# One 64x64 block-diagonal stationary tile for two 32-row quarters in the small levels of a triangular inversion

## The reference

```python
A = jnp.where(tri, 0.0, -jnp.einsum('bhncd,bhned->bhnce', kb, k))     # layer 0; kb = k * beta
for i in range(1, chunk):
    upd = jnp.einsum('...k,...kj->...j', A[..., i, :], A[..., :, :i])
    A = A.at[..., i, :i].add(upd)
inv = A + jnp.eye(chunk, dtype=A.dtype)                               # inverse of a unit lower triangular matrix
u, w = inv @ v, inv @ kb
# then chunk by chunk: out = q S + attn (u - w S);  S = S + k^T (u - w S)
```

## Time and profile before

| | |
|---|---|
| median of 3 runs | 6088.86 us |
| lowest and highest run | 6067.7 and 6097.42 us |
| span of the profiled execution, first to last instruction | 6065.7 us |
| instructions in it | 101127 |
| mean granted TensorE clock, of full speed | 0.739 |
| busy: PE, PEld, DVE, ACT, POOL | 66%, 50%, 54%, 32%, 13% |

### The profile page before, as it was taken

The page is one execution under the profiler, slowest core; times in us unless marked ns, Lnnn a source line. Parts: engine busy times, 40 slices in busy tenths (PEclk is TensorE's granted clock), DMA queues, the critical chain, the costliest instruction groups (busy, mean ns, idle before and its releaser), DMA issues.

```text
span 6065.7 us, 101127 instructions
## 1 busy us (share of the span) xinstructions
PE 4010.7 (66%) x42763; PEld 3031.6 (50%) x42812; DVE 3278.0 (54%) x8153; ACT 1942.4 (32%) x4236; POOL 818.4 (13%) x600
## 2 busy tenths in 40 slices
PE   5565656367778787755475665657767677766288
PEld 4454535255555555544353544534444445445277
DVE  6776867425555555565446455455565555555332
ACT  2233231223333333311313233234444444442122
POOL 0000000231111111124200000011111111110444
PEclk6555555588898988866666666668887788778599
DMA  9000000140000000011200000000000000000255
GB/s 256 15 2 1 2 1 2 61 143 1 1 1 1 1 1 1 1 35 19 47 2 1 2 1 1 2 1 1 1 1 1 1 1 1 1 1 1 66 160 142
DMA packets 140741, 148.57 MB, mean 24 GB/s; under 512 B 7792, under 2 KB 127986, under 8 KB 139776
## 3 DMA queue, kind: packets, MB, share of 16 engines
q1 hardware_dynamic: 118880, 124.05, 7.0%
q0 software_dynamic: 21408, 18.05, 1.8%
HBM read 83.22 MB, written 59.76 MB: 24 GB/s over the span
## 4 chain that ended last, share of the span: by engine, by line
PE 43%; DVE 35%; ACT 12%; issue 6%; POOL 2%; DMA 2%; another core or an unknown queue 1%; SPq 0%; DVEq 0%; POOLq 0%; ACTq 0%
DVE weights L1215 4%; ACT work L3162 4%; PE banks_lane L422 3%; PE banks_lane L3599 2%; PE banks_lane L1818 2%; PE banks_lane L3004 2%; PE banks_lane L3048 2%; DVE weights L3255 1%; PE banks_lane L933 1%; ACT work L1912 1%; PE banks_lane L3083 1%; DVE work L2725 1%; PE banks_lane L793 1%; PE banks_lane L3070 1%; PE banks_lane L1876 1%
## 5 line engine op out<-in xcount | busy, mean ns | idle before, releaser
L422 PE MATMUL banks_lane<-constants,weights 128*128 128x128 f32 x724 | 154.3, 358 | 492.7 <-DVE weights L408 135.2
L422 PE MATMUL banks_lane<-constants,work 128*128 128x128 f32 x840 | 171.1, 351 | 356.8 <-DVE work L408 195.0
L422 PEld LDWEIGHTS banks_lane<-constants,weights 128*128 128x128 f32 x724 | 111.6, 184 | 532.5 <-issue 170.9
L402 POOL TENSOR_TENSOR weights<-weights,constants 128x4 f32<-128x4 f32 x80 | 82.6, 1033 | 2169.4 <-DVE weights L397 2169.4
L1215 DVE SCALAR_TENSOR_TENSOR weights<-weights 128x1024 f32<-128x1024 f32 x268 | 342.4, 1278 | 6.8
L422 PEld LDWEIGHTS banks_lane<-constants,work 128*128 128x128 f32 x840 | 132.3, 182 | 423.4 <-DVE work L408 185.4
L3162 ACT ACTIVATE work<-banks_lane,weights 128x192 f32<-128x192 f32 (+1 forms) x512 | 248.6, 499 | 245.6 <-DVE weights L3259 245.6
L3267 POOL TENSOR_TENSOR weights<-weights,constants 128x16 f32<-128x16 f32 x64 | 185.5, 2898 | 530.8 <-DVE weights L3175 530.8
L402 POOL TENSOR_TENSOR work<-work,constants 128x4 f32<-128x4 f32 x72 | 73.4, 1020 | 1171.0 <-DVE work L397 1171.0
L3083 PE MATMUL banks_lane<-constants,work 128*128 128x128 f32 x896 | 149.6, 316 | 120.5 <-DVE work L3247 70.8
L1965 DVE TENSOR_REDUCE work<-banks_lane 128x2 f32<-128x512 f32 x256 | 158.8, 683 | 67.6 <-PE banks_lane L1832 67.2
(11 more groups left out here) (795 smaller groups left out, 10922.9 us busy)
## 6 DMA issues: line engine op xcount, KB each, us to landing
work<-experts_dram_l_ffn SPq DMA_DIRECT2D x39, 964.0 KB
room_l_ffn<-work SPq DMA_DIRECT2D x30, 1188.0 KB, 14.1
work<-experts_dram_l_ffn SPq DMA_DIRECT2D x23, 512.0 KB
weights<-weights_dram SPq DMA_DIRECT2D x1, 4833.5 KB, 14.1
work<-room_l_ffn SPq DMA_DIRECT2D x36, 132.0 KB
weights<-weights_dram SPq DMA_DIRECT2D x1, 4112.0 KB, 12.4
weights<-room_l_ffn SPq DMA_DIRECT2D x26, 132.0 KB
weights<-weights_dram SPq DMA_DIRECT2D x1, 3378.0 KB, 10.8
```

The costliest lines, as they stand in the source:

```text
L402: pool.tensor_tensor(n.rstd, n.rstd, c("neghalf", cols=(0, n.rstd.shape[1])), ALU.pow).then_inc(*u.pool.step(name))
L422: done = pe.transpose(bank[0:rows, t * P:(t + 1) * P], block, c("ident"))
```

## The change

In levels 1 to 4 two neighbouring quarters share one stationary tile of 64x64, whose two off-diagonal 32x32 blocks are zero. A product is then, for each of the 8 matrices, two matmuls instead of four. The moving operand stays 32 columns wide in the left product and 16 in the right one, but covers 64 partitions. `strict` gets its own storage, 512 columns, cleared once at the start, with the four copies of `strict_act` going into alternate halves of it. The masked part is written 64 columns wide for each matrix (`part_pair`): the left product's result is read twice by a broadcast, and the masks `small1` to `small4` are 64 wide with zeros where the other quarter lies. Level 0 first adds the two halves of `strict`, one of which is zero on each quarter, to get its 32 columns. Level 5 and 6 are as before.

```diff
-        parts += [(f"small{n}", np.tile(m.T if n == 0 else m, (4, 1)))]
+        parts += [(f"small{n}", np.tile(m.T, (4, 1)) if n == 0 else np.tile(np.kron(np.eye(2), m), (2, 1)))]
...
+def half_of(g):
+    return slice(2 * g * SMALL, 2 * (g + 1) * SMALL)
...
-        self.part, self.strict = (blocks(whole(self.T1)[:, n * small:(n + 1) * small], SMALL) for n in range(2))
+        self.strict = arena.take(INVERTED, 2 * SMALL)
+        self.strict_half = [self.strict[:, :, n * SMALL:(n + 1) * SMALL] for n in range(2)]
+        self.part = blocks(whole(self.T1)[:, 0:small], SMALL)
+        self.part_pair = blocks(whole(self.T1)[:, 0:2 * small], 2 * SMALL)
...
         dve.memset(self.XT, 0.0).then_inc(*u.dve.step())
+        dve.memset(self.strict, 0.0).then_inc(*u.dve.step("strict_cleared"))
...
             for m in range(INVERTED):
-                for q in map(quarter, range(QUARTERS)):
-                    made = pe.matmul(b[2][q, m * SMALL:(m + 1) * SMALL], self.strict[q, m, :], self.x[q, m, :])
+                for g in map(half_of, range(2)):
+                    made = pe.matmul(b[2][g, m * SMALL:(m + 1) * SMALL], self.strict[g, m, :], self.x[g, m, :])
...
             for m in range(INVERTED):
-                for q in map(quarter, range(QUARTERS)):
-                    made = pe.matmul(packed(b[3][q, m * half:(m + 1) * half], n), self.part[q, m, :],
-                                     odd_blocks(self.xt[q, m, :], n))
+                for g in map(half_of, range(2)):
+                    made = pe.matmul(packed(b[3][g, m * half:(m + 1) * half], n), self.part_pair[g, m, :],
+                                     odd_blocks(self.xt[g, m, :], n))
...
-            act.copy(self.strict[quarter(i)], self.NT8[quarter(i), :, quarter(i)]).then_inc(*u.act.step(f"strict{pair}"))
+            act.copy(self.strict_half[i % 2][quarter(i)], self.NT8[quarter(i), :, quarter(i)]).then_inc(*u.act.step(f"strict{pair}"))
...
-        dve.tensor_tensor(self.part, self.strict, per_tile(self.c("small0"), INVERTED), ALU.mult).then_inc(*u.dve.step())
+        dve.tensor_tensor(self.part, *self.strict_half, ALU.add).then_inc(*u.dve.step())
+        dve.wait_ge(*u.dve.last())
+        dve.tensor_tensor(self.part, self.part, per_tile(self.c("small0"), INVERTED), ALU.mult).then_inc(*u.dve.step())
...
-            dve.tensor_tensor(self.part, of_heads(b[2], INVERTED * SMALL, SMALL), per_tile(self.c(f"small{n}"), INVERTED),
+            twice = of_heads(b[2], INVERTED * SMALL, SMALL).unsqueeze(2).broadcast_to([P, INVERTED, 2, SMALL])
+            own = self.c(f"small{n}").rearrange("p (two n) -> p two n", two=2)
+            dve.tensor_tensor(self.part_pair.rearrange("p m (two n) -> p m two n", two=2), twice,
+                              own.unsqueeze(1).broadcast_to([P, INVERTED, 2, SMALL]),
                               ALU.mult).then_inc(*u.dve.step(f"part{pair}_{n}"))
```

## The result

The changed kernel takes 6134.67 us in the median of 5 runs (6130.25 to 6136.85), against 6088.86 us for the kernel before (5 runs, 6067.7 to 6100.74). The ratio is 1.0079, 95% interval 1.0064 to 1.0094: slower by 46 us between the medians, where the forecast was slower by 40.

What follows compares the result with a forecast made beforehand. VectorE was taken to bound layer 0's stretches, instruction fetch layer 2's. Layer 2 +14.8, layer 0 +23.6 and the start +1.8 gave +40 us, 6129 us on the median 6088.9; range 6096 to 6160.

Steps and rivals of the forecast that it cites:

- A product costs 1.71 us: Levels 1 to 4: 32 matmuls of 64x64 on two places take 1.71 us, twice the old product; bounds 0.86 and 3.42.
- moving columns: Rival: moving columns set matmul spacing, so a product takes 0.86 us; 6058 us in all, chance 0.04.
- places that don't overlap: Rival: the array's two places do not work side by side, 3.42 us a product; about 6460 us, chance 0.05.
- The holes are instruction fetch and go: Layer 2: TensorE's 1.5 us holes are waits for its instructions and vanish; rival that they stay: 6225 us, chance 0.04.
- Layer 2's stretches stay: Layer 2: wider tiles spend the gain from closed holes; +0.1 us a stretch, bounds 0 and +0.8.
- the rival of the risen clock: Layer 2: unbroken work is granted 2.4 GHz, a product takes 0.86 us; 6058 us in all, chance 0.06.
- The prediction's two rows against it: Ten us of 64x64 work and twenty of 128x128 tiles with 32 moving columns stayed at 1.2 GHz.
- Layer 0's masks: Layer 0: masks 512 wide cost +0.26 us each, seven of eight inside a stretch, 1.85 us a stretch.
- Layer 0's gaps: Layer 0: lane 0's addition and first left product add 0.45 + 0.85 us in second pairs; lane 1's addition 0.45 each stretch.
- At the start: Clearing `strict` for two lanes and two layers lies on the path while the stage starts: +1.8 us.
- Layer 2 ahead of each stretch: Layer 2: two additions of 0.45 us and lane 0's longer first left product, +0.85, sum 1.75 us a stretch.
- the costs are half hidden: Rival: additions and wider masks fall into waits, fetch relief reaches further; +15 us, 6104 us in all, chance 0.11.

Runs made afterwards that it cites:

- Run 3: Kernel before with only quarters 0 and 2 in the products of levels 1 to 4, half of these products left out: ratio 0.9864, -83 us.
- run 1: Changed kernel's wide storage, wide masks and addition, but products stay 64 matmuls of 32x32 tiles; against the kernel before: ratio 1.0059, +36 us.
- run 2: 64x64 tiles in the products, but masks 256 wide and no addition, values not the reference's; against the kernel before: ratio 0.9996, -2 us.
- the runs by layer: The change in one layer alone, against the kernel before: layer 0 alone 1.0054, +33 us; layer 2 alone 1.0051, +31 us.
- run 4: Kernel before, but layer 2's left products of levels 2 to 4 use 64x64 tiles from a second copy of `strict` by ScalarE: 6058.05 us, ratio 0.9951.
- 5: The change in layer 0 alone, layer 2 as in the kernel before: ratio 1.0054, +33 us.

## Why the prediction was right, and where it was not

The end is 46 us above the median of before, and the prediction said 40. It added these 40 to the first profile of before (6065.7 us) and then, unchanged, to the median. Against that first profile the changed kernel's span is 67.7 us longer: 31 of these in layer 2, and 13 between layer 0 and layer 2, which the change does not touch. The second profile of before (6086.4 us) is nearest to its median, so the terms are compared with that: 6133.4 - 6086.4 = 47.0 us.

- **A product costs 1.71 us: right.** The row of x32 shows 1.92 us against 1.97 forecast, and the chain 1.70 to 1.72 for one, behind the first. The stationary width sets the spacing and two places overlap. The rivals of moving columns and of places that don't overlap are out. Run 3 shows the same for 32x32 tiles on two places.
- **The holes are instruction fetch and go: right.** 273 packets as forecast, run 3 separates the count from TensorE's time, and each hole ends 2.4 to 2.7 us behind a packet.
- **Layer 2's stretches stay: right.** 278.1 against 276.7 us, +1.4, forecast +0.8.
- **The clock does not rise in them: right.** PE is busy for 34.03 of 34.80 us at a granted clock of 0.50. So the rival of the risen clock is out. The Trainium skill, TensorE: Matmul & The Clock Gate, Part 1: The HAM clock gate, has it that sustained activity gives 2.4 GHz. The trace disagrees for these stretches, by the same row. The prediction's two rows against it were a little less pure than it says: of the 20.7 us about 11 are 128x128 tiles with 32 moving columns, the rest products with 64 or 128.
- **Layer 0's masks: right.** 0.69 us against 0.42, +0.27 each (forecast 0.26), seven in a stretch, 1.9 us. The eight stretches grew by 14.7 us, forecast 14.8 without the additions. Lane 1's addition shows in the gap ahead of the stretch, where these windows are cut.
- **Layer 0's gaps: somewhat low.** Short ones 35.3 to 37.1 (+1.8, forecast 0.45 + 0.85 + 0.45 = 1.75). The long ones rose by 2.7, 0 and 2.4, so the first pair, where I had taken nothing but one addition, pays some of it too. The seven gaps grew by 12.4 in sum; the forecast for them was 4 x 1.75 + 3 x 0.45 = 8.4.
- **At the start: right in size.** The first stretch begins at 82.7 us instead of 80.9, +1.8, and at 84.2 in the changed kernel's second profile. The 1.8 of the forecast were four clearings, of which only two (0.485 us each) lie ahead of layer 0; the other half of what is seen here are the two additions. The clearings ahead of layer 2 can't be told from the variation there.
- **Layer 2 ahead of each stretch: the term that was mis-sized.** I put 1.75 us ahead of each of eight stretches. From the start of the first stretch to the end of the last lie seven gaps, so the forecast for that part is 7 x 1.75 + 0.8 = 13.1 us; it grew from 903.6 to 926.1, by 22.5. The long gaps did as forecast (+5.8 for three, forecast 5.3). The four short ones rose by 15.3 instead of 7.0: the two that lasted 45.6 us by 2.0 each, the two with the early rise, 41.7 and 42.0, by over 5 each. There the changed kernel has neither the early rise nor the second one, which by itself costs 1.2 us (2.5 for 1.3 at the gap's end). So the mis-sized term is the path ahead of the stretches: lane 0's first product was priced at the lower level in both kernels, and the gaps of one execution were read as if their lengths were fixed.
- **The rest**, which the change does not touch, gave back 4.4 us (from layer 0's last stretch to layer 2's first +0.2, behind layer 2's last -4.6). Between the profiles here the stretch of work from layer 0 to layer 2 alone varies from 2020.7 to 2046.5 us, with no order in it, so I count this as no effect of the change.
- **Luck.** The parts that the change touches grew by 51.4 us (1.8 + 14.7 + 12.4 + 22.5) where 40 were forecast; the parts it does not touch gave back 4.4, and the comparison is with one of two profiles of before that lie 21 us apart. That the end is within 6 us of the forecast is in part luck.

That the costs are half hidden is out for layer 0; for layer 2 the runs showed the reverse. The split into parts is less sure than the sum: run 1 gave +36 and run 2 -2 us, 34 together against 46, and the runs by layer gave 64. Each is within about 20 us of the whole, which is what their intervals allow. For the first pair the traces say more: layer 2's short gaps have a mean of 43.4 us before, 43.8 in run 1, 42.8 in run 2 and 47.6 with both. Neither part alone misses the early rise every time; the whole change does. Open stays why the changed kernel always falls on 269.7 us. The runs show that delays of up to 2.3 us don't move it, and its stretches vary by 0.1 us where those with holes vary by 2.6 (33.8 to 36.4 us), so that nothing shakes it off. That the missing variation is what holds it there was argued, not tried: it would take a kernel without holes and with a varying length. The other profiles fit it. Run 3 (no holes) has 242.2 or 242.3 us three times and run 2 (no holes) 265.2 and then 262.9 and 262.8; runs 1, 4 and 5, with holes in layer 2, vary by 3.4, 5.0 and 3.8 us. The five runs of the changed kernel lie within 7 us, those of the kernel before within 33. But run 2 also shows that unbroken stretches alone don't exclude the early rise.

## What to carry to other kernels

Where a run of very small matmuls leaves TensorE with unexplained holes, count its instructions against the packets of the instruction queue before merging tiles: half as many of twice the width only trades one limit for the other, and the best point lies between (run 4), without new work on the engine that bounds another stage (run 1). Price each added instruction in every stage that shares the code. And profile the kernel before twice: a gap whose length hangs on the clock is no fixed number, and idle time put into such a loop may not show at all.

## What was not expected of the hardware

- Removing half of the instructions with TensorE's own time nearly unchanged took a stretch from 34.5 to 23.0 us: a third of it was fetch.
- A loop of 269.7 us took up 2.3 us of added idling without getting longer, by an earlier rise of the clock (10.1 instead of 16.0 us behind the stretch), and 1.15 us with a later first rise (18 us) and a second one.
- 34 us of 64x64 products in an unbroken row, TensorE busy for 98%, were granted 1.2 GHz. In the work behind them, most of it on 128x128 tiles, the clock rose to 2.4 GHz after 10 to 18 us.
